# A change of order in four stages of a two-layer graph network kernel, with one bias product reshaped

## The chip, the cores and the metric

The kernel runs on one core of one Trainium2 chip, as one launch. The metric is the device time of the launch in microseconds (us), lower is better; the median of several launches is compared. The core has five engines with a program of their own each: PE (matrix products), DVE (vector work), ACT (activations and copies), POOL (here casts of weights, gathers and scatters) and SP (here DMA issues only). They meet through semaphores. ACT, SP and POOL each issue DMAs on a queue of their own.

## What is computed

The input is a matrix `x` of 1250 nodes by 512 features and a graph of 21,250 edges with a weight each. Two layers are applied, and each adds three parts to `x`:

```
xn = _layernorm(x)
x = x + _L0_gnn_ref(xn, edges, ...) + _L0_mix_ref(xn, ...)     # 3 SAGE convolutions; linear attention + feed-forward
x = x + _L0_ffn_ref(_layernorm(x), ...)                        # 8 experts of 256, all of them on every row
xn = _layernorm(x)
x = x + _L1_gnn_ref(xn, edge_weight, edges, ...) + _L1_mix_ref(xn, ...)   # softmax messages, a head of two products; attention
x = x + _L1_ffn_ref(_layernorm(x), ...)                        # shared feed-forward + two banks of 8 experts, top-1 routed
```

The places that the change touches compute this:

```
# L0_mix: residual norm, then the first feed-forward
x = _ln(src + attn @ Wo + bo, g1, be1)
ff = relu(x @ W1 + b1) @ W2 + b2
# L1_gnn: softmax of edge weights by source node, and the head
row_sum = segment_sum(exp_e, src)
h = relu(_layernorm(h, gamma, beta))
h = relu(h @ W2 + b2)
# L1_ffn
y = shared(x2)  + bank(x2, "sp") + bank(x2, "fq")    # bank: rows go to their expert, gelu feed-forward, times the gate
```

The output is 1250 by 512 in fp32.

## The kernel before

The 1250 rows are held as ten tiles (`t` 0 to 9) of 125 partitions by 512. Transposed copies, which the products need, are made in three column groups: `GROUPS` is tiles 0 to 3, 4 to 7, 8 and 9 (500, 500 and 250 columns). fp32 products run as three passes over a rounded high part and a low part of each operand (`Hw`, `Lw`, `XH`, `XL`, `HH`, `HL`): ACT writes the high part, DVE subtracts it from the value and writes the low one. Each engine's program is written out by hand, in a function for each, and works off its stages in code order; nothing is scheduled at run time, so a step waits for everything that stands ahead of it on its engine. `MIX` is PE's list of jobs after the attention, which all engines count by.

The stages in order, with the stretch of the span that the profile of before gives them:

- **Edge loop, 77 to 345.** Forty blocks `b` of 32 target nodes build the count and weight tables of the graph. DVE makes a block's one-hot table (L2547), PE multiplies with it (`visit`, L2273), ACT and DVE (`read_block`, L2569) take the result out. Every fourth block, at `b % 4 == 1`, DVE also reduces a finished group of 128 columns: `group_sums` takes its row sum (L2557) and its row maximum (L2558). Rows of the attention's dense products (`turn`, `q`, `k`, `v`, `kv`) are mixed in. In blocks 1, 13 and 25 DVE subtracts the low part of a weight unit (`unit_low`, L2449), which POOL does at other times (L2914 the cast, L2916 the subtraction); the rows of `v` from block 14 on use unit 2.
- **Attention and `wo`, 345 to 392.** Ten tiles of the output projection; after each, DVE adds the row, takes the statistics (`stats`, L1413) and applies the norm of earlier tiles (`norm1`, L1442 and L1444). `heavy_index` (L1512 to L1516), which works out addresses for the most connected nodes for POOL to scatter by, follows tile 3.
- **First feed-forward, 392 to 449.** `t1` turns the normed rows of a group (PE L611), `to_cols` (ACT) and `low_cols` (DVE L1450) take them out, `fu` (jobs 0 to 5, two for each group; PE L629 to L631) is the product with `W1`. `ffn_up` (DVE L1463), `hidden` (ACT) and `ffn_low` (DVE L1469) make its two parts, `t2` turns another ten tiles, and `fd` is the product with `W2` (PE from L618).
- **Three convolutions, the eight-expert feed-forward, the second layer's attention, messages**, to about 1463.
- **Head, 1463 to 1508.** `w1`, then `hd`, ten tiles of the message head: three products each (L969 to L971) and the bias in two products of one row of weights (L973, the high and the low part). `head_rows` (ACT L1355) and DVE (L1455) take the tile out. `root`, `norm_rows` (ACT L1110) and `store_rows` (L1349, a DMA to `d_xg`, from where the experts fetch their rows) follow by groups, then `t7`, the turns for what comes next, and `lg`, the router's logits, to 1517.
- **Shared feed-forward, 1517 to 1556.** `su` and `sd`. As each of the ten rows is complete (`base_ready`) SP stores it to the output (L2847, semaphore `out_stored`). The expert banks are loaded on SP's queue too (L2832): (1, 0) and (1, 2) ahead of the ten stores, (1, 4) and (1, 6) behind.
- **Expert stage, 1557 to 1717.** 34 slot tiles `q` of 128 rows. POOL fetches rows of `d_xg` by index (L2956) four tiles ahead, PE turns them (L3010), makes two products (L3023, L3045) with ACT's gelu between, and POOL adds the result to the output (L2973), which must not start before the ten stores have landed: at `q == 0` POOL waits for `out_stored`.

## Time and profile before

| | |
|---|---|
| three launches | 1715.59, 1720.75, 1721.75 us; median 1720.75 |
| the profiled launch | 1718.81 us |
| its span (first to last instruction) | 1717.1 us |
| mean granted clock of PE | 0.964 of full speed |
| busy time of PE's costliest lines, the dense products L618, L619, L620 | 215.2, 212.9, 212.8 us |
| DMA | 123.93 MB, mean 72 GB/s |

A busy share is an average over stages with different limits. What a changed stage is worth is read at the place: in PE's timeline a gap is printed behind a row in brackets, with the length of the idle time ahead of it and the instruction that ended it. The span and the launch time differ by 1.7 us.

### The profile page before, as it was taken

To read this page: it belongs to the slowest core of one execution; us is meant where nothing else is said; L and a number is where in the kernel's file an instruction comes from. 1 tells how busy PE (TensorE), PEld (TensorE's weight loads), DVE (VectorE), ACT (ScalarE), POOL (GpSimd) and SP (SyncE) were. 2 spreads that over 40 slices of the span, in tenths; PEclk is the share of its full clock that TensorE was granted. 3 is DMA by queue.
4 is the path that set the end of the run, shared out by engine and by line. 5 is a ranking of instruction groups with operands and counts; after the bars stand their busy time and mean duration, and the time that the engine had idled before them with its cause. 6 is when DMAs were issued, how large, how long until landed. Compare 5 with 4: busy or idle time off the path is not lost. (4 is left out here: it accounts for less than half of the span.)

```text
span 1717.1 us, 23796 instructions
## 1 busy us (share of the span) xinstructions
PE 1566.6 (91%) x8993; PEld 1223.8 (71%) x8993; DVE 987.2 (57%) x1767; ACT 445.6 (26%) x853; POOL 303.7 (18%) x191
## 2 busy tenths in 40 slices
PE   3797978797999999999998999998999999897998
PEld 3676767776777877777786787877758755576765
DVE  6878677777964582287246667665154512672332
ACT  3422111122321120121124333335224101351222
POOL 1000002053203022003101121211211000002665
PEclk9899998998999999999998999999999999798999
DMA  4123224351321011002001010100101322447342
GB/s 148 48 67 109 71 92 149 113 154 47 103 85 62 1 44 49 1 35 81 25 1 49 25 50 26 49 25 25 50 18 51 115 87 72 171 176 233 56 84 40
DMA packets 51755, 123.93 MB, mean 72 GB/s; under 512 B 8034, under 2 KB 28409, under 8 KB 44511
## 3 DMA queue, kind: packets, MB, share of 16 engines
q1 hardware_dynamic: 13714, 65.34, 10.7%
q10 hardware_dynamic: 28075, 46.81, 7.8%
q0 software_dynamic: 9856, 10.28, 3.5%
q8 instruction: 74, 1.21, 0.3%
q14 instruction: 36, 0.29, 0.0%
HBM read 92.87 MB, written 40.22 MB: 78 GB/s over the span
## 5 line engine op out<-in xcount | busy, mean ns | idle before, releaser
L618 PE MATMUL ps<-wslot,XH 128*125 128x512 f32 (+2 forms) x560 | 215.2, 384 | 6.6 <-DVE XL L1450 5.0
L619 PE MATMUL ps<-wslot,XH 128*125 128x512 f32 (+2 forms) x560 | 212.9, 380 | 0.0
L620 PE MATMUL ps<-wslot,XL 128*125 128x512 f32 (+2 forms) x560 | 212.8, 380 | 0.0
L2914 POOL CAST wslot<-arena 128x2048 fp32r<-128x2048 f32 x25 | 47.6, 1905 | 804.5 <-PEq L2991 427.1
L629 PE MATMUL ps<-XH,wslot 128*128 128x500 f32 (+1 forms) x336 | 125.3, 373 | 18.7 <-DVE XL L1450 9.2
L1455 DVE TENSOR_TENSOR arena<-ps,arena 125x512 f32<-125x512 f32 x150 | 98.2, 683 | 53.8 <-PE ps L620 47.1
L618 PEld LDWEIGHTS ps<-wslot,XH 128*125 128x125 f32 x560 | 104.9, 187 | 32.8 <-DVE XL L1450 5.9
L2273 PE MATMUL ps<-arena 125*128 x1330 | 95.8, 228 | 32.7 <-DVE arena L2547 29.1
L676 PE MATMUL ps<-CTr,Hhi 125*128 125x500 f32 (+1 forms) x360 | 125.1, 361 | 0.0
L630 PE MATMUL ps<-XH,wslot 128*128 128x500 f32 (+1 forms) x336 | 124.1, 369 | 0.0
L631 PE MATMUL ps<-XL,wslot 128*128 128x500 f32 (+1 forms) x336 | 123.2, 367 | 0.0
L620 PEld LDWEIGHTS ps<-wslot,XL 128*125 128x125 f32 x560 | 104.6, 187 | 22.6
L619 PEld LDWEIGHTS ps<-wslot,XH 128*125 128x125 f32 x560 | 104.9, 187 | 21.9 <-issue 0.2
L2916 POOL TENSOR_TENSOR wslot<-arena,wslot 128x2048 fp32r<-128x2048 f32 x25 | 116.8, 4670 | 2.0
L2273 PEld LDWEIGHTS ps<-arena 125*128 125x128 bf16 x1330 | 83.3, 102 | 40.0 <-issue 39.8
L678 PE MATMUL ps<-CTr,Hlo_head 125*128 125x500 f32 (+1 forms) x324 | 109.8, 353 | 0.0
L2547 DVE TENSOR_SCALAR arena<-arena 125x1280 bf16<-125x1280 int16 x133 | 72.4, 568 | 47.1 <-PE ps L2273 46.4
L629 PEld LDWEIGHTS ps<-XH,wslot 128*128 128x128 f32 x336 | 67.3, 200 | 33.4 <-issue 18.0
L936 PE MATMUL ps<-arena 125*128 125x500 f32 (+1 forms) x240 | 84.6, 514 | 1.4 <-DMA arena<-d_w 1.4
L1504 DVE TENSOR_TENSOR V<-ps,BC 128x500 f32<-128x500 f32 (+1 forms) x36 | 21.3, 592 | 107.3 <-PE ps L682 106.5
L676 PEld LDWEIGHTS ps<-CTr,Hhi 125*128 125x128 f32 x360 | 67.9, 188 | 15.1 <-issue 5.6
L1128 ACT ACTIVATE V<-V,cols 128x500 f32<-128x500 f32 (+1 forms) x96 | 56.0, 631 | 85.5 <-DVE V L1754 85.5
(446 smaller groups left out, 3087.9 us busy)
## 6 DMA issues: line engine op xcount, KB each, us to landing
arena<-in_units SPq DMA_DIRECT2D x29, 1024.0 KB, 4.8
arena<-in_units SPq DMA_DIRECT2D x8, 2048.0 KB, 11.7
d_w<-arena ACTq DMA_DIRECT2D x10, 625.0 KB
d_wt<-arena ACTq DMA_DIRECT2D x10, 625.0 KB, 4.5
rows<-in_rows ACTq DMA_DIRECT2D x22, 256.0 KB, 4.1
d_kv<-V SPq DMA_DIRECT2D x20, 250.0 KB
arena<-d_kv SPq DMA_DIRECT2D x20, 250.0 KB
arena<-d_wt ACTq DMA_DIRECT2D x2, 2441.4 KB
```

The lines of the kernel that those rows point to most:

```text
L618: pe.matmul(o, lhsT=xh[:, k, s], rhs=H4[:, k, 0:nw], start=k == 0, stop=False, skip_group_check=True)
L619: pe.matmul(o, lhsT=xh[:, k, s], rhs=L4[:, k, 0:nw], start=False, stop=False, skip_group_check=True)
L620: last = pe.matmul(o, lhsT=xl[:, k, s], rhs=H4[:, k, 0:nw], start=False, stop=k == K - 1, skip_group_check=True)
L629: pe.matmul(o, lhsT=H4[:, k, f], rhs=XH[:, k, c0:c0 + w], start=k == 0, stop=False, skip_group_check=True)
L630: pe.matmul(o, lhsT=L4[:, k, f], rhs=XH[:, k, c0:c0 + w], start=False, stop=False, skip_group_check=True)
L631: last = pe.matmul(o, lhsT=H4[:, k, f], rhs=XL[:, k, c0:c0 + w], start=False, stop=k == KC - 1, skip_group_check=True)
L676: pe.matmul(o, lhsT=Hhi[0:TP, t, f], rhs=CTr[0:TP, t, c0:c0 + w], start=t == 0, stop=False, skip_group_check=True)
L678: pe.matmul(o, lhsT=Hlo[t][0:TP, f], rhs=CTr[0:TP, t, c0:c0 + w], start=False, stop=False, skip_group_check=True)
L936: last = pe.matmul(o, lhsT=src[:, t, 128 * m:128 * m + 128], rhs=slab_of(i)[:, t, 0:w], start=t == 0, stop=t == NT - 1, skip_group_check=True)
L1455: dve.tensor_tensor(dst, o[0:TP, 0:D], other, ALU.add).then_inc(mx_sem(name), 1)
L2273: last = pe.matmul(ps[:, 3 * (b % 2) + t // 4, 128 * (t % 4):128 * (t % 4) + 128], lhsT=buffer[:, 128 * t:128 * t + 128], rhs=pre_flat[:, ...
L2916: pool.tensor_tensor(wL[unit_slot(u)], wraw, wH[unit_slot(u)].bitcast(F32), ALU.subtract).then_inc(w_ready, 1)
```

## The change

Five things are done.

1. Edge loop: the row maximum of a group is taken at `b % 4 == 3`, two blocks after its row sum; `unit_low` moves from blocks 13 and 25 to 14 and 26.
2. First feed-forward: PE's list becomes `t1` g0, `fu` 0, 1, `t1` g1, `fu` 2, `t1` g2, `fu` 3, 4, 5. On DVE `heavy_index` goes from tile 3 to tile 5, behind two norms, `norm1` starts one tile earlier, and the low parts and the steps of the hidden rows are put in another order; on ACT `hidden(2)` follows the copies of group 2.
3. Head: the two bias products of a tile become one with 64 rows of weights, the high part of the bias in rows 0 to 31 and the low one in rows 32 to 63, against a column of 1/32 (and `ones_r` is written in two copies). On ACT the norms of a group are put between the tiles of `head_rows`, `to_cols` of `t7` comes earlier, and two loads (`b2e`, `b1e`) move, the one ahead of the bias copy, the other behind the logits. DVE takes the low part of `t7`'s group 0 at tile 7.
4. Stores: the ten output stores leave SP's program and queue for ACT's, behind the last gelu of the shared feed-forward.
5. Expert stage: at `q == 0` POOL fetches the rows of tiles 4, 5 and 6 before it waits for the stores; from `q == 3` on it fetches one tile a step as before.

```diff
-MIX = (... + [("wo", t) for t in range(3, NT)] + woven(turned("t1"), by_group("fu", 2)) + all_of("t2", NT) + ...
+MIX = (... + [("wo", t) for t in range(3, NT)] + turned("t1")[0] + [("fu", 0), ("fu", 1)]
+       + turned("t1")[1] + [("fu", 2)] + turned("t1")[2] + [("fu", 3), ("fu", 4), ("fu", 5)] + all_of("t2", NT) + ...
@@ PE, head
-                    for part in (HH, HL):
-                        last = pe.matmul(o, lhsT=ones_r[0:1, 0:1].to_broadcast([1, TP]), rhs=part[0:1, 1, 0:D], start=False,
-                                         stop=part is HL, skip_group_check=True)
-                    last.then_inc(mx_full, 1)
+                    pe.matmul(o, lhsT=ones_r[0:64, 1:2].to_broadcast([64, TP]), rhs=HH[0:64, 1, 0:D], start=False, stop=True,
+                              skip_group_check=True).then_inc(mx_full, 1)
@@ ACT, head
-            head_rows(6, 7)
-            norm_rows(7, 0)
+            norm_rows(7, 0, (0, 1))
+            head_rows(6)
+            norm_rows(7, 0, (2, 3))
             store_rows(0)
-            head_rows(8, 9)
-            act.wait_ge(w_ready, len(UNITS))
-            act.dma_start(b2e, A["b2e"]).then_inc(b2e_loaded, 16)
-            rows_normed(act, 6, NT)
-            act.dma_start(b1e, A["b1e"]).then_inc(b1_loaded, 16)
+            head_rows(7)
+            to_cols("t7", GROUPS[0])
             root(7, 1)
-            to_cols("t7", GROUPS[0])
-            norm_rows(7, 1)
+            norm_rows(7, 1, (4, 5))
+            head_rows(8)
+            norm_rows(7, 1, (6, 7))
             store_rows(1)
+            head_rows(9)
             root(7, 2)
@@ ACT, after the last gelu of su
+            for t in range(NT):
+                act.wait_ge(base_ready, t + 1)
+                act.dma_start(out[TP * t:TP * t + TP, :], R2t[:, t, :]).then_inc(out_stored, 16)
@@ SP
             for e in (0, 2):
                 load_bank(1, e)
-            for t in range(NT):
-                sp.wait_ge(base_ready, t + 1)
-                sp.dma_start(out[TP * t:TP * t + TP, :], R2t[:, t, :]).then_inc(out_stored, 16)
             sp.wait_ge(w_used, len(UNITS))
             for e in (4, 6):
                 load_bank(1, e)
@@ DVE, wo rows and first feed-forward
-                if t == 3:
-                    heavy_index()
                 stats(R2t[:, t, :], t)
+            for t in range(8):
+                row_out(t)
...
+                if t >= 4:
+                    norm1(t - 4)
+                if t == 5:
+                    heavy_index()
+            row_out(8)
+            scales(0, 1)
+            norm1(4)
             low_cols(0, "t1", GROUPS[0])
+            row_out(9)
+            for t in range(5, 8):
+                norm1(t)
             spreads(2)
+            ffn_up(0)
             scales(0, 2)
+            low_cols(0, "t1", GROUPS[1])
             norm1(8)
             norm1(9)
             ffn_up(1)
             ffn_low(0)
+            ffn_up(2)
+            low_cols(0, "t1", GROUPS[2])
             ffn_low(1)
...
@@ DVE, edge loop
             def group_sums(g):
                 own(dve.tensor_reduce(rs[:, g, :], wst[g % 2], X_AXIS, ALU.add))
+
+            def group_tops(g):
                 own(dve.tensor_reduce(rm[:, g, :], CT[:, :, 128 * g:128 * g + 128], X_AXIS, ALU.max))
...
-                if b in (1, 13, 25):
-                    unit_low({1: 1, 13: 2, 25: 3}[b])
+                if b in (1, 14, 26):
+                    unit_low({1: 1, 14: 2, 26: 3}[b])
...
+                if b >= 7 and b % 4 == 3:
+                    group_tops((b - 7) // 4)
@@ POOL, expert stage
-                if q + 4 < 2 * NS:
-                    fetch_rows(q + 4)
+                for f in range(4, 7) if q == 0 else range(q + 4, min(q + 5, 2 * NS)) if q >= 3 else ():
+                    fetch_rows(f)
                 if q == 0:
                     pool.wait_ge(out_stored, 16 * NT)
```

The first place is DVE's program around the `wo` rows. These are the rows of before at tile 3, where the row (L1455) and its statistics (L1413) enclose `heavy_index` (L1512, L1515, L1516):

```order
1017 L1455 TENSOR_TENSOR arena<-ps,arena 125x512
1018 L1413 BN_STATS small<-arena 125x6
1019 L1455 TENSOR_TENSOR arena<-ps,arena 125x512
1020 L1512 SCALAR_TENSOR_TENSOR small<-ps,small 125x10
1021 L1515 TENSOR_SCALAR small<-small 125x10
1022 L1516 COPY small<-small 125x10
1023 L1413 BN_STATS small<-arena 125x6
1024 L1419 BN_AGGR small<-small 125x2 x4
```

The same place in the changed kernel is reached at tiles 4 to 6; L1462 is now the row, L1420 its statistics, L1449 and L1451 the norm, and L1519 to L1523 `heavy_index`:

```order
1029 L1449 SCALAR_TENSOR_TENSOR arena<-arena,small,rows 125x512
1030 L1451 SCALAR_TENSOR_TENSOR arena<-arena,small,rows 125x512
1031 L1462 TENSOR_TENSOR arena<-ps,arena 125x512
1032 L1420 BN_STATS small<-arena 125x6
1033 L1449 SCALAR_TENSOR_TENSOR arena<-arena,small,rows 125x512
1034 L1451 SCALAR_TENSOR_TENSOR arena<-arena,small,rows 125x512
1035 L1519 SCALAR_TENSOR_TENSOR small<-ps,small 125x10
1036 L1522 TENSOR_SCALAR small<-small 125x10
1037 L1523 COPY small<-small 125x10
1038 L1462 TENSOR_TENSOR arena<-ps,arena 125x512
```

`heavy_index` has moved behind two more rows with their statistics, the scales and two norms.

The second place is ACT's program in the head, tiles 6 to 9 of `head_rows` (L1355) with `root` (L1078), the norm (L1110), the copies of `t7` (L1083) and the DMAs. Before:

```order
427 L1355 ACTIVATE ps<-ps,small 125x512 x2
428 L1110 ACTIVATE arena<-arena,small 125x512 x4
429 L1349 DMA d_xg<-arena 125x4x512
430 L1355 ACTIVATE ps<-ps,small 125x512 x2
431 L1372 DMA arena<-in_b2e 96x512
432 L1374 DMA rows<-in_b1e 8x512
433 L1078 ACTIVATE small<-small 125x4
434 L1083 ACTIVATE XH<-ps 128x4x125 x4
435 L1110 ACTIVATE arena<-arena,small 125x512 x4
436 L1349 DMA d_xg<-arena 125x4x512
```

And in the changed kernel, where `head_rows` is L1357 and the store of rows L1351:

```order
429 L1110 ACTIVATE arena<-arena,small 125x512 x2
430 L1357 ACTIVATE ps<-ps,small 125x512
431 L1110 ACTIVATE arena<-arena,small 125x512 x2
432 L1351 DMA d_xg<-arena 125x4x512
433 L1357 ACTIVATE ps<-ps,small 125x512
434 L1083 ACTIVATE XH<-ps 128x4x125 x4
435 L1078 ACTIVATE small<-small 125x4
436 L1110 ACTIVATE arena<-arena,small 125x512 x2
437 L1357 ACTIVATE ps<-ps,small 125x512
438 L1110 ACTIVATE arena<-arena,small 125x512 x2
439 L1351 DMA d_xg<-arena 125x4x512
440 L1357 ACTIVATE ps<-ps,small 125x512
```

The copies of `t7` now stand ahead of the last two tiles, not behind them, and the two loads are gone from here.

The third place is the end of the shared feed-forward. SP's program before:

```order
35 L2825 DMA arena<-in_units 128x2048
36 L2821 DMA BC<-d_heavy 8x1250 x2
37 L2825 DMA arena<-in_units 128x2048 x23
38 L2832 DMA arena<-in_units 128x2x2048 x6
39 L2847 DMA out<-arena 125x512 x10
40 L2832 DMA arena<-in_units 128x2x2048 x2
```

ACT's program in the changed kernel at that time, the last gelus (L1410, L1413), the stores, and the first steps of the expert stage (L3109 copies the first layer's bias columns, L3096 the turned rows, L3104 is the gelu):

```order
464 L1410 ACTIVATE V<-ps,cols 128x250
465 L1413 ACTIVATE HH<-V 128x250
466 L1410 ACTIVATE V<-ps,cols 128x250
467 L1413 ACTIVATE HH<-V 128x250
468 L1416 DMA out<-arena 125x512 x10
469 L3109 ACTIVATE V<-ps 128x68
470 L3096 ACTIVATE V<-ps 128x512 x2
471 L3104 ACTIVATE arena<-ps,V 128x128 x2
```

The ten stores stand between the gelus and the first copy of the expert stage, and SP has the last two bank loads directly behind the others.

## Rows read from the trace of the kernel before

**Rows 1.** The page's first part: busy time, share of the span, instructions.

```profile
PE 1566.6 (91%) x8993; PEld 1223.8 (71%) x8993; DVE 987.2 (57%) x1767; ACT 445.6 (26%) x853; POOL 303.7 (18%) x191
```

**Rows 2.** Windows: length, busy PE, PEld, DVE, ACT, POOL, granted clock, DMA share, GB/s.

```profile
77.00:345.00 268.00, 223.22 (x2564) 197.78 (x2564) 199.51 (x305) 49.87 (x94) 12.76 (x10) 0.94 0.30 98
...
1480.00:1508.00 28.00, 21.84 (x59) 13.47 (x60) 17.66 (x47) 13.44 (x24) 0.00 (x0) 0.51 0.50 187
...
1556.00:1560.00 4.00, 2.39 (x17) 2.13 (x18) 2.37 (x4) 1.19 (x3) 0.23 (x1) 0.91 0.34 131
```

**Rows 3.** PE's waits, 77 to 345: total us, count, longest.

```profile
PE ps L2273 <- DVE arena L2547: 29.1, 21, 3.5
```

**Rows 4.** Timeline of PE in block 26: start, us, instruction, idle time before.

```profile
257.55 1.29 PE L2273 MATMUL ps<-arena 125*128 x20 [3.29 <-DVE arena L2547]
```

**Rows 5.** Timeline of DVE in block 25 of the edge loop.

```profile
250.53 2.28 DVE L2449 TENSOR_TENSOR wslot<-arena,wslot 128x2048 fp32r<-128x2048 f32 x1
...
254.13 1.47 DVE L2558 TENSOR_REDUCE small<-arena 125x10 f32<-125x1280 int16 x1
```

**Rows 6.** Timeline of PE in the first feed-forward.

```profile
395.89 0.65 PE L611 MATMUL ps<-ident,arena 125*128 125x125 f32 x4 [1.86 <-DVE arena L1444]
399.75 0.76 PE L629 MATMUL ps<-XH,wslot 128*128 128x500 f32 x1 [3.21 <-DVE XL L1450]
...
413.98 0.76 PE L629 MATMUL ps<-XH,wslot 128*128 128x500 f32 x1 [4.18 <-DVE XL L1450]
...
424.69 0.35 PE L629 MATMUL ps<-XH,wslot 128*128 128x250 f32 x1 [1.78 <-DVE XL L1450]
...
434.56 0.47 PE L618 MATMUL ps<-wslot,HH 128*125 128x512 f32 x1
```

**Rows 7.** Timeline of DVE at `wo` tile 3 and at the last `ffn_low`.

```profile
376.64 3.03 DVE L1515 TENSOR_SCALAR small<-small 125x10 int32<-125x10 f32 x1
...
429.44 2.74 DVE L1469 TENSOR_TENSOR HL<-V,HH 128x250 fp32r<-128x250 f32 x2
```

**Rows 8.** Timeline of POOL in the same two stretches.

```profile
375.02 4.61 POOL L2916 TENSOR_TENSOR wslot<-arena,wslot 128x2048 fp32r<-128x2048 f32 x1
...
424.75 2.18 POOL L2914 CAST wslot<-arena 128x2048 fp32r<-128x2048 f32 x1 [12.89 <-DVE XL L1450]
427.02 4.56 POOL L2916 TENSOR_TENSOR wslot<-arena,wslot 128x2048 fp32r<-128x2048 f32 x1
```

**Rows 9.** Timeline of PE in the head: tile 6, start of tile 7, turns of group 1.

```profile
1485.03 0.79 PE L969 MATMUL ps<-wslot,HH 128*125 128x512 f32 x1
...
1486.61 0.79 PE L973 MATMUL ps<-HH,ones_r 1*125 1x512 f32 x1
...
1487.75 0.79 PE L969 MATMUL ps<-wslot,HH 128*125 128x512 f32 x1
...
1505.29 3.27 PE L611 MATMUL ps<-ident,arena 125*128 125x125 f32 x16 [4.56 <-ACT arena L1110]
```

**Rows 10.** Timeline of PE in the expert stage: turns of tiles 4, 5 and 6.

```profile
1570.89 0.60 PE L3010 MATMUL ps<-ident,rows 128*128 128x128 f32 x4
...
1583.55 1.12 PE L3010 MATMUL ps<-ident,rows 128*128 128x128 f32 x4 [8.56 <-DMA rows<-d_xg,BC]
...
1588.98 0.60 PE L3010 MATMUL ps<-ident,rows 128*128 128x128 f32 x4
```

**Rows 11.** Timeline of POOL there: scatter of tile 0, fetch of tile 5.

```profile
1572.20 1.83 POOL L2973 DMA_INDIRECT out<-arena,BC  x1 [11.25 <-DVE arena L3148]
1574.34 1.04 POOL L2956 DMA_INDIRECT rows<-d_xg,BC  x1 [0.30 <-issue]
```

**Rows 12.** The page's last part, DMA issues: median us from issue to landing.

```profile
rows<-d_xg,BC POOLq DMA_INDIRECT x34, 3.5
```

**Rows 13.** Timeline of SP's queue: the ten output stores.

```profile
1542.15 18.40 SPq L2847 DMA_DIRECT2D out<-arena  x10
```

**Rows 14.** Timeline of ACT: its first copy of the expert stage.

```profile
1558.45 0.23 ACT L3096 ACTIVATE V<-ps 128x68 f32<-128x68 f32 x1 [22.61 <-PE ps L3033]
```

More of the change, by code:

```diff
@@ L1139, in stream_act @@
             hidden(1)
-            hidden(2)
             to_cols("t1", GROUPS[2])
             load_row("bp0", "bl0")
-            for i in range(3, 6):
+            for i in range(2, 6):
                 hidden(i)
             to_cols("t2", range(NT))
-            act.activation(ones_r[:, :], ones2[:, :], ACT.Copy)
+            act.activation(ones_r[:, 0:1], ones2[:, 0:1], ACT.Copy)
+            act.activation(ones_r[:, 1:2], ones2[:, 1:2], ACT.Copy, scale=1.0 / 32)
             act.wait_ge(heavy_loaded, 32)
@@ L1343, in stream_act @@
             message_high(5)
+            act.wait_ge(w_ready, len(UNITS))
+            act.dma_start(b2e, A["b2e"]).then_inc(b2e_loaded, 16)
             row_ready(act, "gnnb2")
-            act.activation(HH[0:1, 1, 0:D], row("gnnb2")[0:1, :], ACT.Copy).then_inc(hg_high, 1)
+            act.activation(HH[0:64, 1, 0:D], row("gnnb2")[0:64, :], ACT.Copy).then_inc(hg_high, 1)
             def store_rows(g):
@@ L1387, in stream_act @@
                     to_cols("t7", GROUPS[2])
+            rows_normed(act, 6, NT)
+            act.dma_start(b1e, A["b1e"]).then_inc(b1_loaded, 16)
             act.wait_ge(gate_shifted, 2)
@@ L1958, in head_bias_low @@
                 dve.wait_ge(hg_high, 1)
-                own(dve.tensor_tensor(HL[0:1, 1, 0:D], row("gnnb2")[0:1, :], HH[0:1, 1, 0:D].bitcast(F32), ALU.subtract))
+                own(dve.tensor_tensor(HH[32:64, 1, 0:D], rows[32:64, ROW_SLOT["gnnb2"], :], HH[32:64, 1, 0:D].bitcast(F32),
+                                      ALU.subtract))
                 settle()
@@ L2844, in _ @@
                 load_bank(1, e)
-            for t in range(NT):
-                sp.wait_ge(base_ready, t + 1)
-                sp.dma_start(out[TP * t:TP * t + TP, :], R2t[:, t, :]).then_inc(out_stored, 16)
             sp.wait_ge(w_used, len(UNITS))
```

40 lines of the change are left out of this document (16 added, 24 removed).

## The prediction, made before the changed kernel was run

> **What bounds the kernel now.** The first view to read is the share of busy time: PE is busy 1566.6 of 1717.1 us [rows 1], so whatever is gained must come out of the 150 us in which PE waits or out of work taken from PE. Four of the five edits move work of other engines; each can only shorten a wait of PE at its own place, and the waits are therefore read one by one. The second view is the windows. In the edge loop PE is busy 223 of 268 us and DVE 200 [rows 2]; both are near their limit there, and PE's waits for DVE's one-hot table are 29.1 us in 21 pieces, the longest 3.5 [rows 3]. The other places are gaps in PE's timeline: four in the first feed-forward [rows 6], one in the head [rows 9], one of 8.56 us in the expert stage [rows 10]. The granted clock is not full everywhere (0.51 through 1480 to 1508) [rows 2], and the tile behind the long gap of the experts is slower than the next ones, so a gap can cost more than its length.
>
> **Edge loop.** At block 25 DVE runs the low part of a weight unit (2.28 us), the row sum, the row maximum (1.47) and only then the tables [rows 5]; PE's gap behind it is 3.29 [rows 4]. The change takes 2.28 + 1.47 = 3.75 us out of DVE's way there and in block 13, which is more than PE waits, so I credit 3.3 twice, 6.6. Seven other groups lose 1.47 each ahead of PE's visit; but the same instruction returns two blocks later, and DVE, busy 74% of this stretch with PE's waits all put down to it, is not idle between. I credit 0.3 each, 2.1. Unit 2 becomes ready a block later, and the rows of `v` start with it in that very block: I take off 1, about half of the 2.28. That is 7.7, say 8. The bounds: nothing, if DVE's total work alone sets the pace (the change removes none of it); and 9 x 1.47 + 2 x 2.28 = 17.8 if all that moves was pure delay.
>
> **First feed-forward.** The gaps are 1.86, 3.21, 4.18 and 1.78, together 11.03 [rows 6]. Three things in them change. `heavy_index` took 3.03 us on 125x10 numbers [rows 7], and it ended (379.67) when POOL's subtraction of 4.61 from 375.02 ended (379.63) [rows 8]: it was shut out. At tile 5, some 8 us later, POOL has nothing of this kind, so DVE, which sets the pace from 376 to 397, is about 2.8 earlier; PE's own rows leave 2.1 of that for `fu` 0. Next, the low parts of group 1 now stand ahead of two norms, and `fu` 2 alone is set between groups 1 and 2. Going through DVE's new order with its present durations I get `fu` 2 at 409.5 where it is at 413.98, the last gap gone, and the last `fu` ending about 10 us earlier. What speaks against the full 10 is POOL: its cast of 2.18 starts when the last low part of `t1` has been made (12.89 us of waiting for L1450), and the 4.6 us subtraction follows [rows 8]. `ffn_low`, whose two inputs are both in SBUF, met it once already: two of 128x250 took 2.74 us and ended at 432.18 [rows 7], just behind the subtraction's 431.58 [rows 8]. Now that low part comes at about 415, with four `ffn_low` still to come and the turns of `t2`, which covered it, further off. If DVE is shut out until the subtraction ends, at about 423, `fd` starts at 428 and not at 434.56 [rows 6], a gain of 6.5; if not, 10. The lower end is 3, if only the index and one gap go.
> The Trainium skill ("SBUF — State Buffer", Who interferes with whom) says that a DVE instruction with two SBUF inputs contends with a GpSimd instruction that reads SBUF, and that the one who gets the pair first blocks the other fully. The trace agrees at L1469, 2.74 us for the two; by the rule this term is 6.5, without it 10.
> I take 6.5.
>
> **Head.** A tile takes 2.72 us (1485.03 to 1487.75), of which the two bias products are 1.14 (from 1486.61) [rows 9]. One product of 64 rows is not in the trace. Its neighbours are the three products of 128 rows, 1.58 together or 0.53 each, and a bias product of one row, 0.57; so it costs about 0.55 and saves 0.6. If its place in the line is worth nothing extra, up to 1.0. Six tiles lie in the slow stretch: 3.6 to 6. The gap of 4.56 behind the norms of group 1 [rows 9] should shrink, since ACT's copies and half of the norms now stand ahead of the last tiles; but the norms still need the statistics of the last tiles of the group from DVE, which is busy 17.66 of 28 us here [rows 2], and as tiles get shorter DVE's row per tile is what PE meets next. The tiles' gain and the gap's thus can't be added. I take 4; the bounds are 0 (every microsecond goes to DVE or to the normed rows) and 10 (6 + 4.5).
>
> **Stores and expert stage.** PE waits 8.56 for the rows of tile 5, and that tile then takes 5.43 to the next (1583.55 to 1588.98) against the usual 3.94 or so, so the stall costs about 10 [rows 10]. Tile 5 is late because its fetch (1574.34) stands behind the first scatter (1572.20), and that behind 11.25 us of waiting [rows 11] for the stores. With the fetches of 4, 5 and 6 ahead, the first fetch behind the wait is that of 7, behind three scatters: at 1572.20 + about 6 = 1578.2. PE wants tile 7 at 1570.89 + 3 x 3.94 = 1582.7. A fetch lands after 3.5 in the median [rows 12], which would just do; the one behind the first scatter took 9.2 until PE had it [rows 10, 11], which would leave 4.7 of stall and its slow clock. So 10 or 4; I take 7.
> That holds if the stores land no later than now. They were ten issues of 18.40 us in all, from 1542.15 to 1560.55, on SP [rows 13], the DMA engines busy 0.34 in 1556 to 1560 [rows 2]. On ACT they compete with bank loads that SP now issues at 1556 and no longer behind them. Each microsecond that they land later costs one. ACT's first copy of the stage ran at 1558.45 after 22.61 idle [rows 14]; in the new kernel it stands behind the ten stores, and if the last one is again issued only at 1560.5, PE's start slips by 2. I keep 7 as the middle of 10 and 4 and count this into the bound: 0 to 10.
> The Trainium skill ("DMA: Bandwidth & Descriptors", Queues, rings and completion order) says that a DMA engine takes turns between the queues that have work for it, packet by packet; by it stores and loads share where before the loads stood behind, and the last store would land later; an estimate by that page is a doubling of the time that its packets take. No trace here shows stores and loads on two queues at this place.
>
> **The sum** is 8 + 6.5 + 4 + 7 = 25.5, against the profiled launch, 1718.81: 1693. The median of the three launches is 2 higher, so 1696 (25 below 1720.75). The four places are far apart and each ends in a stretch that PE bounds, so their gains add.
>
> **Rivals.** A difference of 0.5%, 8.6 us, is about what a measurement of this kernel can tell from none.
> (1) All four places gain about as worked out: 1696, chance 0.50.
> (2) The stores land late, as they share the DMA engines with the last bank loads: for it, the loads now start 4.5 us earlier and on another queue; against it, the low share of 0.34. With the stores 2 later and a fetch that takes 9.2, the stall at tile 7 is 4.7 + 2, with 1.5 of slow clock behind it, and of the 10 only 2 are gained: 1701. Chance 0.18.
> (3) The edge loop is bound by DVE's total, and the moved maxima only move the gaps: for it, every gap there is put down to DVE; against it, DVE is idle 68 us of 268. 1704, chance 0.13.
> (4) DVE isn't shut out in the first feed-forward, and the stall of the experts goes fully: 1696 - 3.5 - 3 = 1689, or less with the head's upper end, 1684. Chance 0.11.
> (5) Gains cancel to under 8.6, by (2) and (3) together with a head that gives nothing and 3 from the feed-forward, some 5 to 8 in all: 1714, chance 0.05.
> (6) Slower: ACT is held by its own ten store issues. For it, they occupied SP's queue for 18.40 us [rows 13], 1.84 each with the waits for the rows, and the experts' first copy and turned rows now stand behind them on ACT. Against it, ACT was idle for 22.61 before that copy [rows 14]. To cancel the rest (25) and be slower by 8.6 the last issue would have to end 34 later than 1558.45, at 1592: 5 us for each of the ten. 1730, chance 0.03.
>
> **How the numbers follow.** The prediction is (1). The range takes in (2), (3) and (4) and leaves (5) and (6) out: 1683 to 1710. Faster by over 0.5% is (1) to (4) less a small tail, 0.90; within 0.5%, 0.06; slower, 0.04.
>
> **What would show it.** In the profile after: PE's waits for the tables in the edge loop fall from 29.1 to about 21, with no gap above 2 behind a group; `heavy_index` takes about 0.2 and not 3.03; the gaps between the `fu` jobs add to under 4, and DVE shows one stretched low part (over 3 us) beside POOL's subtraction; a tile of the head takes about 2.1 where the clock is 0.5; PE has no gap at tile 5, and either none or one under 5 at tile 7; ACT's first copy of the expert stage starts no later behind PE's last `sd` than now. Wrong would be: an edge loop as long as before, which says that DVE's total bounds it; or a stall in the experts as long as before at tile 7, which says that the landing of the stores and not their place decides.

## The result, and the profile after

The changed kernel takes 1703.51 us (median of 4 launches, 1701.44 to 1705.2) against 1719.53 for the one before (1715.59 to 1721.75): ratio 0.9907, 95% interval 0.9889 to 0.9926, that is 13 to 19 us faster, 16 in the middle. Forecast were 25, and 1696; the time lies inside the range of 1683 to 1710. The profiled launch has a span of 1703.0 us at a mean granted clock of 0.969.

The page's first part again, against [rows 1]:

```profile
PE 1554.8 (91%) x8983; PEld 1215.1 (71%) x8983; DVE 989.0 (58%) x1767; ACT 445.3 (26%) x854; POOL 305.7 (18%) x191
```

PE's share is what it was. To see where 14 us of span went, the same instruction was looked up in both timelines of PE and its two start times subtracted:

| PE starts | before | after | earlier by |
|---|---|---|---|
| attention behind the edge loop | 340.46 | 334.62 | 5.8 |
| `fd`, second product of the first feed-forward | 434.56 | 421.19 | 13.4 |
| `hd`, first tile of the head | 1471.03 | 1457.66 | 13.4 |
| `lg`, router logits | 1508.45 | 1487.68 | 20.8 |
| small products (L3033) that open the expert stage | 1557.38 | 1539.27 | 18.1 |
| first product of the expert stage (L3023) | 1559.69 | 1553.76 | 5.9 |
| last row | 1707.31 | 1693.28 | 14.0 |

Three places give 5.8, 7.6 and 7.4 (2.7 of which are lost again in the shared feed-forward); then 12.2 are lost in one place, at the start of the expert stage, and 8.1 won back inside it.

PE's waits in the edge loop, 70 to 345, for the tables (L2558 is the old L2547), against [rows 3]:

```profile
PE ps L2284 <- DVE arena L2558: 22.4, 22, 2.2
```

The total is 6.7 lower and the longest 2.2 where it was 3.5; there are 22 waits where there were 21.

PE's timeline in the first feed-forward, against [rows 6]:

```profile
392.75 0.76 PE L630 MATMUL ps<-XH,wslot 128*128 128x500 f32 x1 [4.10 <-DVE XL L1457]
...
403.62 0.46 PE L630 MATMUL ps<-XH,wslot 128*128 128x500 f32 x1 [2.14 <-DVE XL L1457]
...
417.64 0.65 PE L612 MATMUL ps<-ident,arena 125*128 125x125 f32 x4 [1.64 <-DVE V L1470]
...
421.19 0.77 PE L619 MATMUL ps<-wslot,HH 128*125 128x512 f32 x1
```

`fu` 0 starts 7.0 earlier, and 1.2 of that is new (5.8 were there at the attention). `fu` 2 starts 10.4 earlier, and a new gap stands ahead of the turns of `t2`. DVE's and POOL's timelines say why, one fence each, against [rows 7] and [rows 8]:

```profile
371.88 1.74 DVE L1429 TENSOR_SCALAR small<-small 125x4 f32<-125x4 f32 x1 [0.15 <-DVE small L1426]
...
380.06 0.17 DVE L1522 TENSOR_SCALAR small<-small 125x10 int32<-125x10 f32 x1
...
412.56 4.64 DVE L1476 TENSOR_TENSOR HL<-V,HH 128x500 fp32r<-128x500 f32 x1
417.12 0.47 DVE L1470 TENSOR_SCALAR V<-ps,cols 128x250 f32<-128x250 f32 x1
```

```profile
368.98 4.61 POOL L2929 TENSOR_TENSOR wslot<-arena,wslot 128x2048 fp32r<-128x2048 f32 x1
...
411.80 4.86 POOL L2929 TENSOR_TENSOR wslot<-arena,wslot 128x2048 fp32r<-128x2048 f32 x1
```

`heavy_index` (L1522) takes 0.17 and no longer 3.03. But a step of the statistics (L1429, the old L1422) now stands where `heavy_index` stood, beside POOL's earlier subtraction (368.98 + 4.61 = 373.59), and takes 1.74 where it took 0.17 before: of the 2.86 saved 1.57 are lost again, which leaves the 1.2. The fourth `ffn_low` (L1476) takes 4.64 where the first two take 0.67, and it ends at 417.20, 0.5 behind the end of POOL's subtraction (411.80 + 4.86 = 416.66). The third takes 1.35 (410.90), across the start of that subtraction.

PE in the head, against [rows 9]:

```profile
1468.61 0.79 PE L971 MATMUL ps<-wslot,HH 128*125 128x512 f32 x1
...
1470.18 0.79 PE L974 MATMUL ps<-HH,ones_r 64*125 64x512 f32 x1
...
1470.90 0.79 PE L971 MATMUL ps<-wslot,HH 128*125 128x512 f32 x1
...
1478.22 0.47 PE L971 MATMUL ps<-wslot,HH 128*125 128x512 f32 x1
...
1479.51 0.50 PE L971 MATMUL ps<-wslot,HH 128*125 128x512 f32 x1
...
1484.11 1.80 PE L612 MATMUL ps<-ident,arena 125*128 125x125 f32 x8 [3.22 <-ACT arena L1110]
```

A tile at the low clock takes 2.29 (1468.61 to 1470.90) instead of 2.72. The last two tiles take 1.29 (1478.22 to 1479.51), and the gap ahead of group 1's turns is 3.22 instead of 4.56. A gap of 1.48 ahead of group 0's turns (at 1492.01 before) is gone. The windows of the head show the cause of the 1.29, a granted clock that rises in the stretch of these tiles, where before it was 0.51 over all of it (columns as in [rows 2]):

```profile
1466.00:1475.00 9.00, 8.17 (x16) 4.03 (x16) 8.21 (x22) 5.37 (x11) 0.00 (x0) 0.58 0.61 233
1475.00:1480.00 5.00, 5.00 (x23) 3.87 (x24) 4.08 (x12) 4.36 (x9) 0.00 (x0) 0.73 0.18 59
1480.00:1488.00 8.00, 4.59 (x21) 3.14 (x20) 4.62 (x12) 4.18 (x7) 0.00 (x0) 0.79 0.80 296
```

Of the 2.7 lost in the shared feed-forward, 1.8 are a wait that PE did not have before, for ACT's norm of the last group, which now stands further back in ACT's program:

```profile
1492.53 1.34 PE L612 MATMUL ps<-ident,arena 125*128 125x125 f32 x8 [1.77 <-ACT arena L1110]
```

The large loss is in the next rows. PE at the start of the expert stage (L3036 is the old L3023) waits for ACT's copy of the first turned rows, and later has only a short wait for the rows of tile 7:

```profile
1553.76 3.78 PE L3036 MATMUL ps<-V,arena 128*128 128x128 f32 x16 [12.43 <-ACT V L3096]
...
1578.67 0.66 PE L3023 MATMUL ps<-ident,rows 128*128 128x128 f32 x4 [0.36 <-DMA rows<-d_xg,BC]
```

And this is ACT in that time, from answers for short windows; "ACTq" is its DMA issues, and the time is how long ACT's program was in them:

```profile
1523.87 29.08 ACTq L1416 DMA_DIRECT2D out<-arena  x10
...
1538.40 9.97 ACTq L1416 DMA_DIRECT2D out<-arena  x1
...
1548.41 4.54 ACTq L1416 DMA_DIRECT2D out<-arena  x1
...
1553.00 0.23 ACT L3109 ACTIVATE V<-ps 128x68 f32<-128x68 f32 x1 [35.44 <-issue]
```

The tenth store needs the last row, which DVE's timeline shows complete at 1539.08:

```profile
1538.40 0.68 DVE L2141 TENSOR_TENSOR arena<-ps,arena 125x512 f32<-125x512 f32 x1
```

Still ACT hung in the issue of the ninth store for 9.97 us and of the tenth for 4.54, and only then came to the copy that PE needed. SP had issued its last two bank loads just before the ninth:

```profile
1537.38 0.88 SPq L2848 DMA_DIRECT2D arena<-in_units  x2
```

The windows of the same stretch, the last two columns being the busy share of the DMA engines and GB/s:

```profile
1520.00:1530.00 10.00, 10.00 (x64) 8.83 (x64) 6.51 (x17) 0.00 (x0) 3.25 (x4) 1.00 0.97 388
1530.00:1540.00 10.00, 8.03 (x39) 6.30 (x37) 4.10 (x7) 0.00 (x0) 0.86 (x1) 1.00 0.59 200
1540.00:1550.00 10.00, 1.33 (x11) 1.06 (x10) 1.35 (x2) 0.00 (x0) 2.00 (x2) 0.63 1.00 415
```

The full engines alone do not hold ACT: the first four stores were issued in the first of these windows, at a share of 0.97, in 0.27 to 0.34 each. The slow issues begin with the sixth (2.38).

Theory A: ACT's issues wait for DMA engines that SP's bank loads keep full, and PE waits behind ACT. Rival B: the stores would land late wherever they are issued, and the wait would only show up at another place. Later theory C came in, on the stall that remained.

### The profile page after: what moved, and what is told of

The parts are those of the page before. It is cut to its first block, busy times and chain, and to the rows that moved or that the text cites. A ratio compares the mean times of both kernels' runs of the same rounds, so it can differ in the third digit from the quotient of the medians.

```text
span 1703.0 us, 23777 instructions
## 1 busy us (share of the span) xinstructions
PE 1554.8 (91%) x8983; PEld 1215.1 (71%) x8983; DVE 989.0 (58%) x1767; ACT 445.3 (26%) x854; POOL 305.7 (18%) x191
## 3 DMA queue, kind: packets, MB, share of 16 engines
q1 hardware_dynamic: 12414, 62.78, 10.4%
## 4 chain that ended last, share of the span: by engine, by line
PE 75%; DVE 10%; DMA 7%; ACT 3%; issue 3%; ACTq 1%; POOL 1%; DVEq 0%; SPq 0%; POOLq 0%
PE ps L619 9%; PE ps L620 9%; PE ps L621 9%; PE ps L2284 5%; PE ps L677 4%; PE ps L679 4%; PE ps L630 4%; PE ps L631 4%; PE ps L632 4%; PE ps L938 3%; DMA arena<-d_kv 3%; PE ps L3036 3%; PE ps L3058 3%; PE ps L825 2%; DMA arena<-d_w 2%
## 5 line engine op out<-in xcount | busy, mean ns | idle before, releaser
L630 PE MATMUL ps<-XH,wslot 128*128 128x500 f32 (+1 forms) x336 | 123.2, 367 | 16.2 <-DVE XL L1457 6.2
L1462 DVE TENSOR_TENSOR arena<-ps,arena 125x512 f32<-125x512 f32 x150 | 98.3, 684 | 50.5 <-PE ps L621 45.5
L631 PE MATMUL ps<-XH,wslot 128*128 128x500 f32 (+1 forms) x336 | 121.6, 362 | 0.0
L2284 PE MATMUL ps<-arena 125*128 x1330 | 95.9, 228 | 26.2 <-DVE arena L2558 22.4
L2558 DVE TENSOR_SCALAR arena<-arena 125x1280 bf16<-125x1280 int16 x133 | 72.5, 570 | 47.0 <-PE ps L2284 46.3
L3036 PE MATMUL ps<-V,arena 128*128 128x128 f32 x544 | 69.5, 283 | 14.9 <-ACT V L3096 13.8
```

The lines of the kernel that those rows point to most:

```text
L630: pe.matmul(o, lhsT=H4[:, k, f], rhs=XH[:, k, c0:c0 + w], start=k == 0, stop=False, skip_group_check=True)
L631: pe.matmul(o, lhsT=L4[:, k, f], rhs=XH[:, k, c0:c0 + w], start=False, stop=False, skip_group_check=True)
L2284: last = pe.matmul(ps[:, 3 * (b % 2) + t // 4, 128 * (t % 4):128 * (t % 4) + 128], lhsT=buffer[:, 128 * t:128 * t + 128], rhs=pre_flat[:, ...
L3036: last = pe.matmul(ps[:, 2 + q % 2, ST * m:ST * m + ST], lhsT=w1_of[q][:, k // 2, FF * (k % 2) + 128 * m:FF * (k % 2) + 128 * m + 128], rh ...
```

## The experiments

Each was timed beside the kernel before. "Alone" is one part of the change on the kernel before.

**The parts one at a time.** The edge loop's part (row maxima and the two `unit_low`):

```diff
-                if b in (1, 13, 25):
+                if b in (1, 14, 26):
...
+                if b >= 7 and b % 4 == 3:
+                    group_tops((b - 7) // 4)
```

> The kernel before with the edge loop's part alone (row maximum two blocks later, low parts of units 2 and 3 a block later). Theory: the shift of PE's timeline at the end of the loop, 5 us in the changed kernel, is all its own: 1714 to 1715, ratio 0.997. Rival: the loop's gain is given back in the attention or the first feed-forward, which DVE bounds: under 2 us, ratio 0.999 or more.

Measured: 1712.13, ratio 0.9955 (0.9938 to 0.9972), 8 us and not the 5 of the changed kernel's profile. All of it is there at the end of the loop and nothing is given back (7.5 at the attention, 8.0 at `fd`, 8.1 at the end). PE's waits for the tables are those of the changed kernel:

```profile
PE ps L2273 <- DVE arena L2547: 22.3, 22, 2.2
...
PE ps L2188 <- DVE wslot L2449: 1.4, 1, 1.4
```

The second row is the price, unit 2's low part a block later, waited for once by the rows of `v`.

The `wo` rows and the first feed-forward:

```diff
-MIX = (... + [("wo", t) for t in range(3, NT)] + woven(turned("t1"), by_group("fu", 2)) + all_of("t2", NT) + ...
+MIX = (... + [("wo", t) for t in range(3, NT)] + turned("t1")[0] + [("fu", 0), ("fu", 1)]
+       + turned("t1")[1] + [("fu", 2)] + turned("t1")[2] + [("fu", 3), ("fu", 4), ("fu", 5)] + all_of("t2", NT) + ...
...
+            for t in range(8):
+                row_out(t)
```

> The kernel before with the part of the wo rows and the first feed-forward alone. Theory: 8 us (PE's timeline moved from -5 to -13 between 374 and 434 in the changed kernel and kept 7 of them), 1712, ratio 0.9955. Rival: part of that came from the edge loop's earlier end (POOL's subtraction falls elsewhere): 4 or less alone, 1716.

Measured: 1713.07, ratio 0.9951 (0.9937 to 0.9965), 8 us. In the profiled launch `fd` starts at 428.45. DVE's fourth `ffn_low` is stretched here as well, beside POOL's subtraction, which runs from 419.39 to 424.25, so this part owes nothing to the loop's earlier end:

```profile
420.15 4.63 DVE L1470 TENSOR_TENSOR HL<-V,HH 128x500 fp32r<-128x500 f32 x1
```

The head's part, and of it the bias product alone:

```diff
+                    pe.matmul(o, lhsT=ones_r[0:64, 1:2].to_broadcast([64, TP]), rhs=HH[0:64, 1, 0:D], start=False, stop=True,
+                              skip_group_check=True).then_inc(mx_full, 1)
```

> The kernel before with the head's part alone, the one bias product of 64 rows and ACT's and DVE's order. Theory: PE reaches the expert stage 5 to 6 us earlier and the kernel ends as much earlier, 1714, ratio 0.997. Rival: the stores or the bank loads set when the expert stage can go on, and the stall of 8.56 at tile 5 grows by what the head gains: no change, 1719 to 1720.

> The kernel before with one edit of the head alone: the two bias products of one row become one of 64 rows. Theory (PE's products set the tile's time at the low clock): a tile at the low clock goes from 2.72 to 2.1 us or less, the kernel gains 2 to 4. Rival (DVE's row per tile or the copies of ACT set it): the tiles get shorter on PE but PE's wait for the norms of group 1, 4.56, grows by the same, gain under 1.

Measured: 1715.69 for both edits together, ratio 0.9973 (0.9962 to 0.9983), and 1715.61 for the bias product alone, 0.9978 (0.9962 to 0.9994). The two intervals overlap almost fully, so what the new order on ACT and DVE adds isn't shown by the times. The traces put `lg` 8.7 earlier with both and 4.7 with the product alone, of which 1.3 and 1.1 were there ahead of the head; PE's timeline of the bias product alone shows the norms of group 1 waited for about as long as before, 4.98 against 4.56:

```profile
1483.21 0.79 PE L969 MATMUL ps<-wslot,HH 128*125 128x512 f32 x1
...
1485.50 0.79 PE L969 MATMUL ps<-wslot,HH 128*125 128x512 f32 x1
...
1500.63 3.39 PE L611 MATMUL ps<-ident,arena 125*128 125x125 f32 x16 [4.98 <-ACT arena L1108]
```

So in the head itself both edits gain 7.4 and the product alone 3.6; the order's 3.8 is to be seen there (the wait is 3.22 with it, and the 1.48 ahead of group 0's turns, which the product alone keeps, is gone). But at the first product of the experts the two kernels are 5.1 and 4.8 earlier than before: what the order gains is lost again. With the order PE waits 1.74 for ACT's norm of the last group (at 1504.58), as in the changed kernel; with the product alone it has no such wait. Another 1.2 go at the start of the expert stage, at a granted clock of 0.53 (1551.0 to 1554.5).

POOL's fetches:

```diff
-                if q + 4 < 2 * NS:
-                    fetch_rows(q + 4)
+                for f in range(4, 7) if q == 0 else range(q + 4, min(q + 5, 2 * NS)) if q >= 3 else ():
+                    fetch_rows(f)
```

> The kernel before with POOL's edit alone: the rows of tiles 4, 5 and 6 are fetched before the wait for the stores. Theory: PE's wait of 8.56 us at tile 5 goes, or shrinks to under 3 at tile 7, and the kernel gains 6 to 9, 1712. Rival: the stores land so late (POOL's first scatter at 1572) that the stall only moves to tile 7 at 4 to 5 us: gain 3 to 5.

Measured: 1714.62, ratio 0.9973 (0.9962 to 0.9984), 5 us. The rival was right: the stall is at tile 7 instead of 5 and 3.71 long instead of 8.56.

```profile
1586.58 1.12 PE L3010 MATMUL ps<-ident,rows 128*128 128x128 f32 x4 [3.71 <-DMA rows<-d_xg,BC]
```

The stores:

```diff
@@ ACT, after the last gelu of su
+            for t in range(NT):
+                act.wait_ge(base_ready, t + 1)
+                act.dma_start(out[TP * t:TP * t + TP, :], R2t[:, t, :]).then_inc(out_stored, 16)
```

> The kernel before with the move of the ten stores from SP to ACT alone. Theory A: ACT is held by its issues, PE waits 10 to 14 us for ACT's first copy, but the stall of 8.56 at tile 5 is swallowed by it in part, and the kernel takes 2 to 6 more than before, 1722 to 1726. Rival (the late start replaces the stall exactly, or ACT isn't held where the rest of the kernel is as before): within 2 us of before.

Measured: 1724.75, ratio 1.0030 (1.0017 to 1.0042), 5 us slower. The ten issues took 28.76 on ACT, the ninth alone 9.49, PE waited 11.10 at the first product, and POOL's first scatter waited for the last store until 1582.29, ten later than before. The stall of 8.56 was swallowed.

```profile
1571.82 3.39 PE L3023 MATMUL ps<-V,arena 128*128 128x128 f32 x15 [11.10 <-ACT V L3083]
```

```profile
1582.29 1.64 POOL L2973 DMA_INDIRECT out<-arena,BC  x1 [20.66 <-DMA out<-arena]
```

Those five ratios (loop, feed-forward, head, fetches, stores) add to 1 - 0.0045 - 0.0049 - 0.0027 - 0.0027 + 0.0030 = 0.9882; measured together 0.9907 (0.9889 to 0.9926). The difference of 4 us is no larger than what the intervals of the parts leave open together.

**The stores back on SP**, all the rest of the change kept:

> The changed kernel with one part undone: the ten output stores are back on SP, between the bank loads (1, 2) and (1, 4). Theory A (ACT was held by its own store issues, 29.08 us for ten, and PE waited 12.43 us for ACT's first copy of the expert stage): that wait goes, the copy starts within 2 us of PE's turns, and the kernel takes 10 to 12 less than the changed one, about 1692. Rival B (the stores land late wherever they are issued from, since the bank loads fill the DMA engines, and POOL's first scatter waits for them): the wait moves to the first scatter and to tile 7, and the kernel stays at 1700 to 1704.

Measured: 1699.05, ratio 0.9880 (0.9865 to 0.9895). The expected 1692 was not reached. PE's timeline shows both theories in part: the wait of 12.43 is gone (the first product at 1539.94, 19.8 earlier than before), and a wait of 6.98 stands at tile 7, whose fetch POOL issued at 1560.88:

```profile
1568.68 1.12 PE L3023 MATMUL ps<-ident,rows 128*128 128x128 f32 x4 [6.98 <-DMA rows<-d_xg,BC]
```

**The stores on ACT with the loads held** tells whether it is ACT's queue or the traffic:

```diff
-            for e in (0, 2):
-                load_bank(1, e)
+            load_bank(1, 0)
+            sp.wait_ge(out_stored, 16 * NT)
+            load_bank(1, 2)
```

> The changed kernel with its stores on ACT, but SP holds the last three bank loads, (1, 2), (1, 4) and (1, 6), until the ten stores have landed. Theory A1 (ACT's issues are slow because the DMA engines take turns between ACT's stores and SP's 8 MB of loads): the ten issues take under 18 us in all, PE's wait of 12.43 falls under 3, the kernel takes 8 to 12 less than the changed one. Rival A2 (ten such stores in a row always fill ACT's own queue): ACT's issues still take 25 us or more and the wait stays at 10 or above.

Measured: 1698.87, ratio 0.9882 (0.9864 to 0.9901), 4 to 5 less than the changed kernel and not the 8 to 12 expected. ACT's ten issues now take 16.31, and nothing waits for its copy. Both spans hold waits for the rows to be complete. The issues by themselves add to 22.7 in the changed kernel and to 7.2 here; the ninth and tenth take 1.75 and 0.89 instead of 9.97 and 4.54. So it is the loads that make them long, and rival A2 falls by its own sign (25 or more). It keeps a small part: even with the loads held, late stores of the ten take up to 1.75 to issue, against 0.28 for the first. How the loads hold an issue, by the taking of turns that A1 names or otherwise, is not shown. Tile 7 is stalled again:

```profile
1521.97 16.31 ACTq L1416 DMA_DIRECT2D out<-arena  x10
```

```profile
1571.32 1.12 PE L3024 MATMUL ps<-ident,rows 128*128 128x128 f32 x4 [7.31 <-DMA rows<-d_xg,BC]
```

**The stores on SP, ahead of load (1, 2)**, with the two lines swapped:

> The changed kernel with the stores back on SP, but ahead of bank load (1, 2) and not behind it. Theory A (ACT must be free, and the stores must land early): no long wait at the start of the expert stage and none at tile 7, 1 to 4 us less than with the stores behind (1, 2), about 1690. Rival: behind (1, 2) the stores land in time anyhow, both the same within 1 us; or the bank load comes too late for the second bank, which would show as a wait of PE at its first tile, near 1625.

Measured: 1698.21, ratio 0.9878 (0.9857 to 0.9899), the same as behind it within the intervals, as the rival said. POOL's first scatter came at 1552.25, 2.5 earlier than with the stores behind the load, and still the stall was there, longer. The fetch was issued at 1558.15 and took 12.7 until PE had it; the DMA engines were full up to 1560 and busy 0.80 from there to 1571:

```profile
1570.85 1.12 PE L3023 MATMUL ps<-ident,rows 128*128 128x128 f32 x4 [8.56 <-DMA rows<-d_xg,BC]
```

```profile
1550.00:1560.00 10.00, 10.00 (x67) 7.71 (x66) 2.88 (x4) 3.04 (x7) 6.06 (x4) 1.00 1.02 391
```

So an early landing of the stores doesn't remove it. From this came theory C, that a fetch is late because it shares the DMA engines with the bank loads; D, that it is late because of the wait for the stores. Three kernels, the third with load (1, 2) behind the stores as above, hold the last two loads until PE has turned ten tiles:

```diff
             sp.wait_ge(w_used, len(UNITS))
+            sp.wait_ge(xt_full, 10)
             for e in (4, 6):
                 load_bank(1, e)
```

On the changed kernel with the stores on SP, on the kernel before, and with the stores on ACT:

> The changed kernel with the stores on SP behind bank load (1, 2), as in the run of 1699, and the last two bank loads held until PE has turned ten tiles of the expert stage. Theory C (the remaining stall of 7 us at tile 7 is a fetch that shares the DMA engines, busy 0.97 between 1550 and 1560, with 4 MB of bank loads): the stall falls under 2 and the kernel takes 5 to 8 less, about 1692. Rival D (the fetch is late since POOL issues it behind three scatters that waited for the stores): the stall stays at 4 or more, 1696 to 1699. If the loads then come too late, PE waits before tile 17.

> The kernel before with one line more: the last two bank loads are held until PE has turned ten tiles of the expert stage. Theory C: of the 8.56 us that PE waits for tile 5, the part that is the fetch's own time falls from 9.2 to about 4 and the stores land earlier too, so the wait falls under 4 and the kernel takes 4 to 7 less, 1714. Rival D: the stores, not the loads, hold the fetch; the wait stays over 7 and the time at 1719 to 1720.

> The changed kernel with its stores on ACT, load (1, 2) held until they have landed and the last two bank loads until PE has turned ten tiles. Theory A1 with C: ACT's issues take 16 to 18 us as with all three loads held, PE has neither the wait of 12.43 nor one above 2 at tile 7, and the time is within 2 us of the same with the stores on SP, about 1692. Rival: ACT's queue costs something of its own, which shows as 3 us or more above the stores on SP.

Measured: 1699.86, ratio 0.9883 (0.9865 to 0.9901); 1722.26, ratio 1.0012 (1.0001 to 1.0024); 1700.27, ratio 0.9891 (0.9877 to 0.9905). None is faster than the same kernel without the hold. PE's timeline of the kernel before with the hold shows why:

```profile
1576.24 1.11 PE L3011 MATMUL ps<-ident,rows 128*128 128x128 f32 x4 [4.72 <-DMA rows<-d_xg,BC]
...
1610.03 1.12 PE L3011 MATMUL ps<-ident,rows 128*128 128x128 f32 x4 [5.72 <-DMA rows<-d_xg,BC]
```

SP issued the held loads here:

```profile
1596.60 0.92 SPq L2832 DMA_DIRECT2D arena<-in_units  x2
```

The stall of 8.56 at tile 5 falls to 4.72, and a new one of 5.72 comes 13 us behind the loads. With the stores on SP it is the same: a wait of 3.09 at tile 7, then 1.07 at 1583.30 and 4.99 at 1592.80, behind loads of 1578.80.

On the cause C is right. From POOL's issue of the late fetch to PE's turn of its rows, it takes 4.0 to 5.0 us in the three kernels with the hold (and 4.4 in the changed kernel, where the fetch of tile 7 comes at 1574.32, long after the loads), and 7.7 to 12.7 in the kernels with the loads in flight (9.2 before, 7.7 with the fetches alone, 7.8 with the stores back on SP, 11.8 with the loads held only until the stores had landed). On what follows from it C is wrong: in the first two kernels PE's waits for fetches, over the whole stage, add to 11.9 and 9.8 us, against 9.5 and 7.3 without the hold, and come to more. With the stores on ACT and the hold, the ten issues took 16.41, there was no wait for ACT, and tile 7 was waited for only 0.27, as expected. There the waits for fetches add to 6.0, against 9.4 without the hold. But the expected 1692 was not reached, and the median is not lower than without the hold (1698.87).

What remains of the first stall comes with no loads in flight (a DMA share of 0.18 in 1565 to 1572), and POOL's timeline of the kernel before with the hold shows it as D says, the scatter that waits for the stores and the fetch of tile 5 behind it:

```profile
1570.33 1.64 POOL L2974 DMA_INDIRECT out<-arena,BC  x1 [11.14 <-DMA out<-arena]
1572.27 1.05 POOL L2957 DMA_INDIRECT rows<-d_xg,BC  x1 [0.30 <-issue]
```

PE was free for tile 5 at 1571.52 (1576.24 less 4.72), before its fetch was issued at all.

## Why the prediction held, and what was mis-sized

**Edge loop: 8 forecast, 8 measured alone** (5 to 11), and 5.8 in the changed kernel's one profile. The mechanism is as written: the waits for the tables add to 22.4 where about 21 was forecast, none is longer than 2.2, and unit 2's later low part is waited for once, 1.4 us where 1 was taken off. Rival (3), DVE's total, falls. But the two blocks with a weight unit, 3.3 us each in the sum, do not carry it. The gap of 3.54 at 169.80 became 0.91, and 1.37 of that came back in the wait for unit 2. The one of 3.29 at 257.55 became two of 0.86 and 2.23, and behind it PE was 1.7 ahead (275.48 against 277.14) where it had been 2.4 ahead in front of it (246.59 against 249.02). The last 4 us came behind that, 2.8 of them at two of the groups credited 0.3 each: the gap of 2.00 at 306.97 became 0.61, that of 3.40 at 330.03 became 2.01. The total of this term is right, its parts are not. These are rows of PE's timeline, before and after:

```profile
169.80 2.11 PE L2273 MATMUL ps<-arena 125*128 x20 [3.54 <-DVE arena L2547]
...
330.03 1.92 PE L2273 MATMUL ps<-arena 125*128 x20 [3.40 <-DVE arena L2547]
```

```profile
168.40 1.29 PE L2284 MATMUL ps<-arena 125*128 x20 [0.91 <-DVE arena L2558]
...
260.74 2.31 PE L2284 MATMUL ps<-arena 125*128 x20 [2.23 <-DVE arena L2558]
...
324.42 2.31 PE L2284 MATMUL ps<-arena 125*128 x20 [2.01 <-DVE arena L2558]
```

The size from one profile is uncertain by some 3: the seven profiled kernels that hold this part come to the attention at 329.2 to 335.1 (the middle one at 333.3), the seven that don't at 338.6 to 342.1 (the middle one at 339.4), which is 6 between the middle ones.

**First feed-forward: 6.5 forecast, 8 measured alone** (6 to 11). The steps came as worked out: `heavy_index` at 0.17 and not 3.03; `fu` 2 at 403.62 in the changed kernel, which is 409.4 without the 5.8 of the loop, where 409.5 had been forecast; the stretched `ffn_low`, at 4.63, ending just behind POOL's subtraction at 424.25 where 423 had been forecast. Two sizes were off. `fu` 0 gained 1.2 and not 2.1, since the statistics took part of `heavy_index`'s wait. And `fd` at 428.45, where 428 had been forecast, agrees by luck: that profile comes to the attention 1.7 later than the one before (342.13 against 340.46), so the part moved `fd` by 7.8, as in the changed kernel (7.6), and not by 6.1. The sign "under 4" for the gaps between the `fu` jobs fails if the gap ahead of `fu` 0 counts, as it did in the 11.03: 0.26, 4.10 and 2.14 make 6.5. Rival (4)'s half about DVE not being shut out falls.

**Head: 4 forecast, 5 measured alone** (3 to 7). The product of 64 rows saved 0.43 a tile at the low clock, less than the 0.6 taken, so a tile took 2.29 and not 2.1: it costs 0.72 (1470.18 to 1470.90) where 0.55 had been estimated and one row cost 0.57. Over the four tiles at the low clock that is 1.7. The first four ran at the higher clock in both kernels, 1.3 instead of 1.5, and the last two ran at the higher clock, 1.29 instead of 2.7; neither was in the sum. The gap shrank by 1.3 only (3.22), since DVE's statistics come ahead of the norms, as written; the 1.48 ahead of group 0's turns and the new 1.77 ahead of the last group's were not in the sum either. So 4 and 5 agree in part by luck. The order's own share is not shown by the times.

**Stores and expert stage: 7 forecast, nothing in the end, and this is the step that failed.** The prediction had both halves in hand and priced one wrongly. The fetches were worth 5 alone, between the 10 and the 4 that had been worked out, with the stall at tile 7 at 3.71 where 4.7 was the bad case. But I wrote "if the last one is again issued only at 1560.5, PE's start slips by 2" and "I keep 7 as the middle of 10 and 4 and count this into the bound: 0 to 10". The issues on ACT did not take SP's 18.40 but 28.76 to 29.08, and PE's start slipped by 12. The move alone costs 5, and in the changed kernel PE reached the stage 18.1 earlier, which is what the other three terms had promised (8 + 6.5 + 4 = 18.5), and finished it 14.0 earlier, a term of -4, outside the bound. The sign that ACT's first copy would start no later behind PE's last `sd` than before failed plainly, 16.1 (1536.91 to 1553.00) against 3.25; the sign on tile 7 came true (0.36), but only because PE itself came there late. Rival (6) named this mechanism and gave it 0.03, because it asked only from which size it would turn the whole sum; a mechanism that speaks for itself at a third of that size should have stood in the sum. Its duration was taken from SP's row, where the loads stood in the same queue, and not asked again for two queues. That the whole time still fell inside the range rests on the width of the range.
The Trainium skill's rule on turns between queues ("DMA: Bandwidth & Descriptors", Queues, rings and completion order) had been set beside the sum with the landing of the stores as what would suffer. The runs agree with it on the landing: POOL's first scatter waited for the last store in the move alone until 1582.29, against 1572.20 before. The loss that counted was another one, that the issue itself took longer, 28.76 against 16.31 with the loads held, and that was not worked out from the rule.

**The sum.** 8 + 8 + 5 + 5 - 5 is 21, and 16 (13 to 19) was measured for all. With the stores on SP the four others sum to 25.5, which is what was forecast for everything, and 21 (18 to 23) were measured. The four intervals together leave some 4.6 open and that of the whole 2.6, so what is lacking, 5, is hardly clear of noise. One place where parts overlap is seen in the profiles: the wait at tile 7 was 6.98 with all parts and 3.71 with the fetches alone. From the small products to the end of the span the expert stage took 159.7 before, 155.0 with the fetches alone, 156.1 with the stores back on SP and 163.7 in the changed kernel; four kernels with the stage as it was before took 160.7 to 163.2, so these lengths are uncertain by some 3 as well.

The five versions in which PE doesn't wait for ACT take 1698 to 1700 and can't be told from each other. Against the changed kernel's 0.9907 (0.9889 to 0.9926) they stand at 0.9878 to 0.9891; the intervals still overlap at their ends, so that putting the stores back is worth 4 to 5 rests on both this and the move alone, which is clear of no change.

## What to carry to other kernels

A DMA issue is work of the engine that issues it: before moving stores to an engine with idle time, look at the busy share of the DMA engines in that stretch, at how many stores follow each other, and at what stands behind them in that engine's program. The first four stores of 250 KB took 0.3 us each to issue at a share of 0.97; the ninth, at 1.00, held its engine for 10 us.
When a stall is a fetch that comes late among bulk loads, moving the loads among later fetches can move the stall with them; compare the sum of the waits and the time, not the wait at the old place.
A mechanism that can't turn the sign still has a price at its likely size, and that belongs in the sum.

## What the runs showed of the hardware

The issue of one store on ACT's queue took 9.97 us while SP's queue had bank loads in flight (1540 to 1550: 415 GB/s, a DMA share of 1.00). The ten issues with the waits for their rows took 16.31 in all with three loads held and 28.76 to 29.08 with them; the issues by themselves 7.2 and 22.7. The first four took 0.27 to 0.34 each even at a share of 0.97.

An indirect fetch took 4.0 to 5.0 us from its issue to PE's use with the loads held, and 7.7 to 12.7 with loads in flight.

At the low clock, from start to start and with 512 columns, a bias product of 64 rows took 0.72, one of a single row 0.57 and the products of 128 rows beside them 0.53 on average (0.59, 0.42 and 0.56): the time did not follow the number of rows.

A DVE subtraction of 128x500 with both inputs in SBUF took 4.63 to 4.64 beside a POOL subtraction and 0.67 while POOL was idle, in two kernels alike.
